# A transformer of twelve stages on one core: which constants the first norm awaits, where the first queries stand, and how two routers and the first expert's rows are ordered

## What is computed

```python
def _layernorm(x, axis):                 # ahead of every sublayer
    ...
# L0_ffn: 8 experts, 2 per token, weights renormalised, no capacity
# L2_xattn: 16 heads of 64; q, k, v from normed x and normed context
    q = _split_heads(Qn @ wq, B, Nq)
    k = _split_heads(Kn @ wk, B, Nk)
    v = _split_heads(Vn @ wv, B, Nk)
    qn = _l2norm(q)
    kn = _l2norm(k)
    attn = jnp.einsum('bhqd,bhkd->bhqk', qn, kn)
    out = jnp.einsum('bhqk,bhkd->bhqd', attn, v)
# L2_ffn: 8 experts, 2 per token, at most C rows for each expert
    gates = jax.nn.softmax(xf @ Wg.T, axis=-1)
    topw, topi = jax.lax.top_k(gates, K)
    C = int(round(K * T * CAP_RATIO / E))
    ...
    cnt = jnp.take_along_axis(jnp.cumsum(oh, 0) - oh, e_ord[:, None], 1)[:, 0]
    within = cnt < C
    pos = jnp.where(within, cnt, C)
```

## Time and profile before

| | |
|---|---|
| median of three runs | 2631.78 us (2630.09 to 2638.85) |
| the profiled execution | 2638.47 us, its span 2637.1 us |
| PE busy | 2356.0 us (89%) |
| DVE, ACT, POOL busy | 1207.8, 924.0, 573.2 us |
| mean granted clock of PE | 0.942 of full speed (2.4 GHz) |
| DMA | 224.29 MB, mean 85 GB/s |

### The profile page before, as it was taken

One profiled execution on the slowest core, in us unless ns is written; L12 is line 12 of the kernel. 1 busy time (PEld: TensorE's weight loads), 2 busy tenths in 40 slices (PEclk: granted clock), 3 DMA queues, 4 the chain that ended last, 5 costly groups with the idle time before them and its releaser, 6 DMA issues. The chain is left out here.

```text
span 2637.1 us, 34511 instructions
## 1 busy us (share of the span) xinstructions
PE 2356.0 (89%) x13630; PEld 1598.1 (61%) x13630; DVE 1207.8 (46%) x2321; ACT 924.0 (35%) x2500; POOL 573.2 (22%) x587
## 2 busy tenths in 40 slices
PE   6885999998998999786899999689995899989999
PEld 5674777767675665223466656668883478744555
DVE  5644222255787473656234431410006566677442
ACT  2211222242674461554232232022222456434331
POOL 1621222232001011201354420033312100043110
PEclk9977999999999899898899999789997999989999
DMA  5015888840001000200000000322315833210000
GB/s 167 0 33 219 302 303 301 301 157 1 1 2 53 1 2 32 100 1 32 0 1 1 0 1 0 112 73 93 98 45 202 327 148 139 81 36 1 9 9 17
DMA packets 75383, 224.29 MB, mean 85 GB/s; under 512 B 9359, under 2 KB 52757, under 8 KB 65238
## 3 DMA queue, kind: packets, MB, share of 16 engines
q1 hardware_dynamic: 67894, 204.82, 21.4%
q0 software_dynamic: 7328, 17.26, 1.9%
HBM read 178.68 MB, written 45.17 MB: 85 GB/s over the span
## 5 line engine op out<-in xcount | busy, mean ns | idle before, releaser
L221 PE MATMUL psum<-arena 128*128 128x256 f32 (+4 forms) x3716 | 987.5, 423 | 16.1 <-ACT arena L231 3.9
L221 PEld LDWEIGHTS psum<-arena 128*128 128x128 f32 (+1 forms) x3716 | 681.3, 186 | 279.8 <-issue 130.1
L263 POOL TENSOR_SCALAR x_moments<-x_moments 128x4 f32<-128x4 f32 x48 | 12.5, 260 | 879.9 <-DVE x_moments L256 879.5
L1964 DVE TENSOR_REDUCE small<-psum 128x4 f32<-128x1024 f32 (+1 forms) x112 | 137.0, 1223 | 116.4 <-PE psum L1875 65.6
L1234 POOL DMA_INDIRECT l_out<-arena,slot_tables x79 | 78.6, 996 | 412.4 <-ACT arena L1412 234.0
L1937 ACT ACTIVATE arena<-psum,small 128x128 f32<-128x128 f32 (+1 forms) x384 | 148.8, 414 | 51.5 <-DVE small L1964 51.3
L3555 PE MATMUL psum<-arena 128*128 128x512 bf16 x768 | 166.2, 379 | 0.0
L1439 DVE TENSOR_TENSOR arena<-arena,psum 128x352 f32<-128x352 f32 x78 | 40.6, 521 | 253.7 <-ACT arena L1390 253.7
L1975 DVE COPY arena<-psum 128x512 f32<-128x512 f32 x224 | 143.5, 680 | 1.7 <-PE psum L1886 1.5
L1870 PE MATMUL psum<-arena 32*128 32x128 f32 (+1 forms) x1280 | 133.1, 339 | 0.0
L1937 ACT ACTIVATE z<-psum,small 128x128 f32<-128x128 f32 (+1 forms) x256 | 103.8, 426 | 74.8 <-DVE small L1964 74.8
(11 more groups left out here) (360 smaller groups left out, 3480.9 us busy)
## 6 DMA issues: line engine op xcount, KB each, us to landing
arena<-L_ffn_w_in SPq DMA_DIRECT2D x39, 2176.0 KB
arena<-L_ffn_W_in SPq DMA_DIRECT2D x16, 1024.0 KB
positions<-arena SPq DMA_DIRECT2D x16, 1024.0 KB, 5.2
arena<-positions SPq DMA_DIRECT2D x16, 1024.0 KB, 7.8
arena<-l_out SPq DMA_DIRECT2D x16, 512.0 KB, 7.7
positions<-arena SPq DMA_DIRECT2D x16, 512.0 KB, 5.2
arena<-positions SPq DMA_DIRECT2D x16, 512.0 KB, 8.5
arena<-ctx_in SPq DMA_DIRECT2D x2, 2048.0 KB, 10.3
```

Source lines behind the costliest of these rows:

```text
L221: last = nc.tensor.matmul(out, lhsT, rhs, start=(n == 0), stop=(n == len(pairs) - 1))
L1964: nc.vector.reduce_max(self.minus_top(h), use.bank(u).rearrange("p (h l) -> p h l", l=L), AX_X, negate=True).then_inc(self.topped.up(), 1)
```

## The change

Four parts.

1. *Start.* GpSimd no longer writes `minus_half`; ScalarE does, as its first operation. The first norm waits for x alone (PE for ident, GpSimd for `minus_half`); tables and head_scale are awaited behind it.
2. *Routers.* The tile's one-hot has a signal, and ScalarE makes the second of the two products with it. The choice's number is split at 128 instead of 64, so that the second part is the same in all columns of a partition and can be ScalarE's scale. In L2Mixture, two operations that need only the chosen experts stand ahead of the counts.
3. *L2Mixture's first expert.* Each of its five gathers has a semaphore. PE transposes three tiles, makes four of the hidden products of the first half, transposes the other two tiles and goes on.
4. *L2Cosine.* The queries of sequence 0 come ahead of the context's transposes. They hold banks 0 to 3, and the context's transposes use 4 and 5 for even groups, 6 and 7 for odd ones. ScalarE's squares and VectorE's units of these queries stand ahead of those of the keys.

```diff
@@ Router.pe, act, dve, invert
         bank, N = use.take(self.use_rows), 2 * TILES
+        pe.wait_ge(self.places_in)
...
         self.norm.act_zT(GROUPS - 1)
+        self.k.act.wait_ge(self.tiles_in)
+        self.k.nc.scalar.activation(self.parts[:, :, self.tiles:2 * self.tiles], self.tile_hot, ACT.Copy,
+                                    scale=self.k.choice_parts[1][:, 0:1]).then_inc(self.places_in.up(), 1)
...
+        if self.capacity is not None:
+            dve.wait_ge(self.chosen)
+            dve.step(nc.vector.tensor_tensor(place3, hot3, k.count_up[:, 0:E].unsqueeze(1).to_broadcast([P, 32, E]), ALU.mult))
+            dve.step(nc.vector.reduce_sum(base, place3, AX_X))
         dve.wait_ge(*use.filled(self.use_counts))
...
-        for n, part in enumerate(k.choice_parts):
-            nc.vector.tensor_tensor(self.parts[:, :, tiles * n:tiles * n + tiles], high,
-                                    part.unsqueeze(2).to_broadcast([P, N, tiles]), ALU.mult)
+        dve.wait_ge(self.tiles_in)
+        nc.vector.tensor_tensor(self.parts[:, :, 0:tiles], high, k.choice_parts[0].unsqueeze(2).to_broadcast([P, N, tiles]),
+                                ALU.mult)
@@ L2Cosine
-        self.ctx_turn = Turn(k, u, self.normed, self.cT, TILES, scale=g1, bias=b1n)
+        self.ctx_turn = Turn(k, u, self.normed, self.cT, 0, scale=g1, bias=b1n)
...
+        self.q_use.extend(u.add("sums", 2) for _ in range(2))
+        for g in range(GROUPS):
+            self.ctx_turn.use.append([u.add(engine, 1, 4 + 2 * (g % 2) + c) for c, engine in enumerate(("dve", "act"))])
         context()
-        queries()
@@ L2Cosine.pe
+        self.norm.pe_zT(0)
+        for mark in self.norm.zT_in(0):
+            pe.wait_ge(*mark)
+        self.pe_queries(0)
         for g in range(GROUPS):
             self.ctx_turn.pe(g, (self.ctx_normed, 4 * g + 4))
...
         self.pe_context(0)
-        self.pe_queries(0)
@@ L2Cosine.act, dve
+        self.act_square(self.unit("q", 0, 0), self.q_use[0])
         for g in range(GROUPS):
             self.ctx_turn.act(g)
         self.norm.act_zT(GROUPS - 1)
+        self.act_square(self.unit("q", 0, 1), self.q_use[1])
...
+        self.dve_queries(0)
         self.dve_context(0)
-        self.dve_queries(0)
@@ L2Mixture
+    def pe_turn_first(self, part):
+        use, tiles = self.uses, (range(self.FIRST), range(self.FIRST, self.RT))[part]
+        for a in tiles:
+            self.k.pe.wait_ge(self.first_rows[a])
+        for c in range(DC):
+            u = self.turn_use[0][2 * part + c]
+            self.turned(0, use.take(u), c, tiles).then_inc(use.fills(u), 1)
...
+                    if (e, half, m) == (0, 0, MT // 2):
+                        self.pe_turn_first(1)
@@ begin
-    constants, tables_in = k.loads("constants_loaded", 3), k.counter("constants_set", "pool").reserve(3)
+    ident_in, constants = k.loads("ident_loaded", 1), k.loads("constants_loaded", 2)
+    tables_in, half_in = k.counter("constants_set", "pool").reserve(2), k.counter("half_set", "act").reserve(1)
...
-    nc.gpsimd.memset(k.minus_half, -0.5).then_inc(tables_in.up(), 1)
-    for q in (k.pool, k.act, k.dve, k.pe):
-        q.wait_ge(constants)
-        q.wait_ge(tables_in)
+    k.act.wait_ge(tables_in)
+    nc.scalar.activation(k.minus_half, k.ones_wide[:, 0:TILES], ACT.Identity, scale=-0.5).then_inc(half_in.up(), 1)
+    k.pool.wait_ge(half_in)
+    k.pe.wait_ge(ident_in)
...
         first.norm.dve_final(g, (x_loaded[g], 1))
+    for q in (k.pool, k.act, k.dve, k.pe):
+        q.wait_ge(constants)
+        q.wait_ge(tables_in)
+        q.wait_ge(ident_in)
+        q.wait_ge(half_in)
```

More of the change, by code:

```diff
@@ L1098, in dve @@
         by_expert, bank = "p (e n) -> p e n", use.bank(self.use_counts)
+        place3, hot3 = place.rearrange("p (n e) -> p n e", e=E), hot.rearrange("p k i e -> p (k i) e")
+        over, base = scratch[:, 32:64], scratch[:, 64:96]
+        if self.capacity is not None:
+            dve.wait_ge(self.chosen)
+            dve.step(nc.vector.tensor_tensor(place3, hot3, k.count_up[:, 0:E].unsqueeze(1).to_broadcast([P, 32, E]), ALU.mult))
+            dve.step(nc.vector.reduce_sum(base, place3, AX_X))
         dve.wait_ge(*use.filled(self.use_counts))
@@ L1164, in invert @@
         dve.wait_ge(*use.filled(self.use_rows))
-        dve.step(nc.vector.tensor_scalar(number, bank[:, 0:tiles], 64.0, -1.0, ALU.mult, ALU.add))
+        dve.step(nc.vector.tensor_scalar(number, bank[:, 0:tiles], float(P), -1.0, ALU.mult, ALU.add))
         nc.vector.tensor_tensor(number, bank[:, tiles:2 * tiles], number, ALU.add).then_inc(use.empties(self.use_rows), 1)
@@ L1203, in rows_shared @@
         self.rows_ring = ring
-        self.rows_loaded = [k.loads(f"rows_loaded{n}", per * len(range(n, blocks, ring))) for n in range(ring)]
+        self.rows_loaded = [k.loads(f"rows_loaded{n}", per * len(range(n, blocks, ring)[n < apart:])) for n in range(ring)]
+        self.apart = apart
         self.y_stored = [k.loads(f"y_stored{n}", per * len(range(n, blocks, 2))) for n in range(2)]
@@ L1223, in store_rows, with gather @@
                                 k.z[:, 4 * g:4 * g + 4, :]).then_inc(self.z_stored.up(), 16)
-    def gather(self, j, out, n, count=P):
+    def gather(self, j, out, n, count=P, loaded=None):
         k = self.k
@@ L2645, in __init__, with unit @@
         self.renormed = k.counter("z_normed_again", "dve").reserve(GROUPS)
+    def unit(self, what, b, a):
+        return 4 * b + a + (0 if (what == "q") == (b == 0) else 2)
     def pe_rows(self, u, w, srcT, i):
@@ L2764, in act @@
         act.wait_ge(self.fetch.loaded)
+        self.norm.act_zT(0)
+        self.act_square(self.unit("q", 0, 0), self.q_use[0])
         for g in range(GROUPS):
@@ L2823, in dve_context @@
         for a in range(2):
-            self.dve_unit(4 * b + a, self.kn[b % 2][:, a, :], self.k_use[2 * b + a], free)
+            self.dve_unit(self.unit("k", b, a), self.kn[b % 2][:, a, :], self.k_use[2 * b + a], free)
     def dve_queries(self, b):
@@ L2828, in dve_queries @@
         for a in range(2):
-            self.dve_unit(4 * b + 2 + a, self.qn[b % 2][:, a, :], self.q_use[2 * b + a], free)
+            self.dve_unit(self.unit("q", b, a), self.qn[b % 2][:, a, :], self.q_use[2 * b + a], free)
     def dve_renorm(self, g):
@@ L2841, in dve @@
         dve.wait_ge(self.fetch.loaded)
+        self.norm.dve_zT(0)
         for g in range(GROUPS + 1):
@@ L2941 @@
 class L2Mixture(Mixture):
+    FIRST = 3
     def __init__(self, k):
@@ L2966, in __init__ @@
         self.folded = k.counter("same_row_made", "pool").reserve(1)
-        self.turn_use, self.h_use, self.y_use, self.strip_use = [[u.add("dve", 2), u.add("act", 2)]], [], [], []
+        self.turn_use, self.h_use, self.y_use, self.strip_use = [[u.add("dve"), u.add("act")]], [], [], []
         for e in range(E):
-            self.h_use.append([[u.add("act") for _ in range(MT)] for _ in range(2)])
+            self.h_use.append([[], []])
+            for half in range(2):
+                for m in range(MT):
+                    if (e, half, m) == (0, 0, MT // 2):
+                        self.turn_use[0] += [u.add("dve"), u.add("dve")]
+                    self.h_use[e][half].append(u.add("act"))
             if e + 1 < E:
@@ L2976, in __init__ @@
         self.ring = [k.loads(f"expert_weights{n}", E) for n in range(2)]
-        self.rows_shared(RT, E)
+        self.rows_shared(RT, E, 2, 1)
+        self.first_rows = [k.loads(f"first_rows{a}", 1) for a in range(RT)]
     def count(self, a):
@@ L3087, in load_rows @@
                 n = self.count(a)
-                self.gather(e, self.rows[e % 2][0:n, a, :], self.RT * e + a, n)
+                self.gather(e, self.rows[e % 2][0:n, a, :], self.RT * e + a, n, None if e else self.first_rows[a])
     def pool(self):
```

63 lines of the change are left out of this document (36 added, 27 removed).

## The result

The changed kernel takes 2622.2 us (median of six runs, 2620.67 to 2623.15), the kernel before 2634.71 us beside it (2630.09 to 2639.33). The two medians lie 12.5 us apart. The ratio on record is 0.9944 (95% interval 0.993 to 0.9958), which is 14.8 us less, 11 to 18. The direction is as forecast. The time is 10.2 us above the forecast of 2612 and 0.2 above the end of the range.

The account below looks back on a forecast made before the run. TensorE, busy 2356.0 of 2637.1 us, was taken as the bound, leaving only its waits to win. Terms 7.0 + 3.7 + 2.8 + 6.2 = 19.7 us, taken from the median 2631.78, gave 2612 us; range 2603 to 2622.

Parts of the forecast that it names:

- What bounds the kernel: Whole kernel: TensorE is busy 2356.0 of 2637.1 us, so only the remaining 281 us of waits can be won.
- The start: First stage: norm waits for x alone (5.8 us) and the table load moves early (1.2 us), 7.0 us saved.
- The routers: L0Mixture and L2Mixture routers: one product moves to ScalarE, two operations ahead of the counts; 1.4 and 2.3 us saved.
- The first expert: L2Mixture: hidden products start 3.4 us earlier, late transposes cost 0.5 us; net 2.8 us saved.
- L2Cosine: First queries fill a 10.20 us idle stretch; context products 1.6 us later, normalising units start earlier; 6.2 us saved.
- warm-clock rival: L2Cosine: shorter idle time keeps PE at 2.4 GHz before the transposes; 3 us more gain, 2609 us; chance 0.10.
- What a stage start wins is kept until the end: Long stages between: semaphore chains carry each gain to the end, unless a DMA started at a fixed time intervenes.
- none of the terms depends on that difference: Sum: the median of three runs, 6.7 us below the profiled execution, can serve as base for the 19.7 us.
- Gated start: First stage: weights or context hold the second half at the old time; gain 12.7 us, 2619; chance 0.10.
- no gain in L2Cosine: Units take 7 us instead of 5.58, delaying the key-value product; gain 13.5 us, 2618; chance 0.14.
- a stall in the later sequences: L2Cosine: the 6.93 us stall returns in seven later sequences, about 9 us each; 2675 us; chance 0.03.
- Less than it says: Whole change: two of the four parts hidden elsewhere, gain under 8 us, about 2626; chance 0.08.

Follow-up runs that it names:

- the two tests: Kernel before against the changed kernel (2622.2 us), and the changed kernel with L2Mixture's first expert waiting for five gathers again (2622.2 us).
- the four tests: Changed kernel with one part undone at a time: start 2625.17 us, L2Cosine 2625.19, L2Mixture's first expert 2622.2, routers 2622.65.
- The second execution: The kernel before, unchanged, run and traced again: 2631.77 us.
- the delayed kernels: Changed kernel with two, four or six copies of x ahead of VectorE's first statistics: 2619.98, 2621.06 and 2623.29 us.

## Why the prediction was right, and where it was not

**What bounds the kernel** held: PE's busy time is the same, and the microseconds came out of waits at the places named.

**The start**: 6.3 to 6.4, forecast 7.0. The chain is as described. The landing of x was taken at 5.5 (1.2 + 4.3) and VectorE started at 5.94, 0.44 later. That is one execution: in the five other traces with this start and no added copies VectorE started at 5.16 to 5.38, and in four of them the spectra stood at 21.98 to 22.19, in the fifth at 20.62. In the three traces with the old start they stood at 29.16 to 29.36. So the term is 7.0 to 7.4 in those four, and what is missing in after is a late landing. The drain of 1.38 us that the Trainium skill ("ScalarE: Activation LUTs", What ACT_TABLE_LOAD costs) adds to a table load is not in the result: the load in after ends at 2.01 us and the operation behind it starts at 2.03. With the drain the term would be 8.4 us, an estimate from that page's figure and my 7.0, and taking the start back cost 6.4.

**The routers**: L0Mixture 1.1 to 1.2 (forecast 1.4), L2Mixture 2.3 (forecast 2.3). The ScalarE product took 1.34 us (1.25), and VectorE's one-hot released PE, as said.

**The first expert**: 2.6 and 2.5 in the two tests, forecast 2.8. The two halves are 3.4 (3.4) and -0.8 (-0.5): four late transposes cost 0.87 us in PE's row, where I had taken half of 0.26 each.

**L2Cosine**: 5.75 and 5.1, forecast 6.2. Sixteen queries end at 1235.1 on the old time (forecast 1235.3); the context products lose 1.65 (1.6); the key-value product comes at 1281.6 (1281.4), idle 6.70 before it (about 6). It took 3.68 us where I had taken 3.2, which is the missing 0.5. The warm-clock rival was half there: the first eight transposes began at 1232.12, the granted clock fell at 1232.7, and they took 1.45 us, between the 1.94 of half clock and the 1.09 of full clock. It did not matter, since group 2 waited for a copy and not for the clock.

**What failed** is the step that turned the sum into a time, in two sentences. "What a stage start wins is kept until the end": the lead fell and rose in stages that nobody touched, by up to 3.9 us (9.3 at 640 us, 5.45 at 720) and by -1.6 in all, and in the four tests what was left of a local gain at the end of the trace ranged from nothing (-0.2 of 2.5) to all of it (6.8 of 6.4). And "none of the terms depends on that difference" (of 6.7 us between the profiled execution and the median). The median of three was the time of a lucky group: of the 30 runs of before in all comparisons, 11 lie at 2630.1 to 2632.3 and 19 at 2637.6 to 2641.4, none between. In the two large comparisons every run of before with a granted clock of 0.944 or 0.945 is in the lower group and every one with 0.942 or 0.943 in the upper. The second execution, which is in the lower group, shows the 6.7 us as clock steps in unchanged code. After has all its six runs within 2.5 us, at 0.944 or 0.945, so the gain is 9.2 us against the lower group and 17.6 against the upper. The forecast took the median of one group and the terms from a trace of the other. On the trace's own basis it is 2618.8 against 2621.99: 3.2 us off, half of it in the terms (1.6) and half at the clock (1.6). That this makes up the whole gap is arithmetic; why after has no upper group in its six runs is not shown. The range, too, was cut short: its upper sum is 2619.4, the 4 us named beside it lead to 2623.4, and it was put down as 2622.

**The rivals.** Gated start and no gain in L2Cosine are refuted by the rows above, and a stall in the later sequences by the lead, which is 11.98 us at 1320 us and 11.94 at 1550. "Less than it says" is false place by place.

## What to carry to other kernels

Find each gain where it stands by pairing the products of two traces; differences of a few us in the end time say little for a kernel like this, since the start was worth 6.4 us locally and 3.0 in the median, and the first expert's rows 2.5 and nothing. Before forecasting a median, look whether the runs of before form groups, and work from the group to which the profiled execution belongs. When a buffer or bank is given to new work, look for the copy that frees the remaining ones: here it stood behind norm work that it did not need, and moving it, together with q's units, gave 6.4 us in L2Cosine, as much as the largest part of the change.

## What the hardware showed that I had not expected

One program on one core has two groups of times about 8 us apart (2631.4 and 2639.9 on average), and of the 6.6 us between the traces of one member of each, 5.9 arise where PE stands at 1.2 GHz in the one and at 2.4 in the other. A kernel with 0.62 us of added copies in its first stage ended 2.0 us earlier. Sixty-four key-value products of 64 columns took 2.09 us at full clock and 3.5 to 3.7 us at half clock, also after a wait of only 2.34 us. The load of x, issued at the same 1.20 us in after and in the delayed kernels, was seen by VectorE at 5.21 to 5.94 us. What decides at which instruction the clock rises again stays open.
